# Biases of two mixtures of experts: from turned gates to a row of ones, a third output bank and a GpSimd add

## The reference, cut to what matters

```python
# first layer's mixture: 4 experts, 256 hidden, gates sum to 1 over two experts
for ei in range(4):
    g = jnp.where(topk_i == ei, w, 0.0).sum(-1)
    hh = gelu(x @ W1[ei] + b1[ei])
    out = out + g[..., None] * (hh @ W2[ei] + b2[ei])
...
# second layer's mixture: 8 experts, 256 hidden, two gates of eight are not zero
h = gelu(xf @ w1 + bb1)
y = h @ w2 + bb2
acc = acc + we[:, None] * y
```

## Time and profile before

| what | us |
|---|---|
| median of 3 runs (lowest 3353.7, highest 3367.92) | 3366.84 |
| the profiled execution | 3369.89 |
| its span, first to last instruction | 3368.1 |
| its front | 0 to 1171 |
| its last program | 1268 to 3368 |
| mean granted TensorE clock, share of full | 0.859 |

### The profile page before, as it was taken

One profiled execution on the slowest core, in us unless ns is written; L12 is line 12 of the kernel. 1 busy time (PEld: TensorE's weight loads), 2 busy tenths in 40 slices (PEclk: granted clock), 3 DMA queues, 4 the chain that ended last, 5 costly groups with the idle time before them and its releaser, 6 DMA issues.

```text
span 3368.1 us, 48945 instructions
## 1 busy us (share of the span) xinstructions
PE 2550.2 (76%) x15405; PEld 1888.7 (56%) x15406; DVE 2449.8 (73%) x7195; ACT 1767.8 (52%) x3180; POOL 1159.6 (34%) x1205
## 2 busy tenths in 40 slices
PE   1789898989889823026887887888878888887899
PEld 0666666767666612014555565665556556555666
DVE  6888888888878646246776866767777686676774
ACT  0566666676667502023555555555555555645654
POOL 0000000000000037656565565565555656556200
PEclk7899999999999955556898888888888988888899
DMA  2011111111111124133332333323233233332300
GB/s 92 32 51 45 54 47 49 54 41 45 47 45 45 53 76 98 34 72 73 79 76 63 85 71 64 91 64 86 66 71 89 63 86 70 81 75 64 83 14 10
DMA packets 228555, 210.48 MB, mean 62 GB/s; under 512 B 70780, under 2 KB 160584, under 8 KB 227656
## 3 DMA queue, kind: packets, MB, share of 16 engines
q1 hardware_dynamic: 190152, 190.84, 19.1%
q0 software_dynamic: 37280, 14.38, 4.8%
q10 hardware_dynamic: 864, 2.14, 0.2%
HBM read 159.49 MB, written 47.74 MB: 62 GB/s over the span
## 4 chain that ended last, share of the span: by engine, by line
DVE 23%; PE 17%; another core or an unknown queue 10%; issue 9%; ACT 3%; POOL 1%; DVEq 1%; DMA 0%; ACTq 0%; POOLq 0%
PE lay_b_y L1798 7%; DVE keep_x L2184 6%; PE lay_b_z L1789 6%; PE lay_b_b L1840 1%; POOL keep_got L1753 1%; DVE lay_oht L2089 1%; DVE lay_stats L2209 1%; ACT lay_unused L2031 1%; DVE lay_split L1093 1%; DVE lay_split L1094 1%; PE lay_b_g L1890 1%; DVE lay_oh L2086 1%; ACT lay_hid L1943 1%; DVE lay_split L1090 1%
## 5 line engine op out<-in xcount | busy, mean ns | idle before, releaser
L1753 POOL DMA_INDIRECT keep_got<-node_table,keep_idx x1143 | 1124.3, 984 | 765.3 <-issue 311.3
L1798 PEld LDWEIGHTS lay_b_y<-lay_w,lay_hid 128*128 128x128 f32 x4096 | 531.7, 203 | 170.2 <-issue 168.2
L1789 PE MATMUL lay_b_z<-lay_xin,lay_w 128*128 128x512 f32 x1024 | 584.9, 700 | 10.6 <-ACT lay_hid L1943 8.1
L1798 PE MATMUL lay_b_y<-lay_w,lay_hid 128*128 128x128 f32 x4096 | 544.4, 286 | 41.9 <-issue 39.1
L2184 DVE SCALAR_TENSOR_TENSOR keep_x<-lay_b_y,lay_gates,keep_x 128x128 f32<-128x128 f32 x1024 | 288.0, 343 | 380.4 <-remote 224.3
L1943 ACT ACTIVATE lay_hid<-lay_b_z,lay_b 128x512 f32<-128x512 f32 x512 | 330.3, 683 | 407.2 <-PE lay_b_z L1789 202.4
L902 POOL MEMSET find_ones<- 128x128 f32 x1 | 0.2, 205 | 1171.4 <-POOLq L49 1171.4
L2031 ACT ACTIVATE lay_unused<-keep_hub_wide,keep_halves 128x1152 bf16<-128x1152 uint16 x256 | 320.3, 1251 | 111.5 <-DMA keep_hub_wide<-sorted_dst 88.9
L1789 PEld LDWEIGHTS lay_b_z<-lay_xin,lay_w 128*128 128x128 f32 x1024 | 202.8, 220 | 178.7 <-issue 156.6
L468 PE MATMUL front_b_h<-front_xt,front_m 128*128 128x512 f32 x512 | 262.3, 643 | 38.2 <-DVE front_hb L719 32.0
L225 DVE TENSOR_TENSOR sort_keys<-sort_keys 128x1024 f32<-128x1024 f32 (+2 forms) x182 | 257.4, 1414 | 21.1 <-ACT sort_keys L548 18.3
(11 more groups left out here) (397 smaller groups left out, 4239.2 us busy)
## 6 DMA issues: line engine op xcount, KB each, us to landing
keep_wide<-sorted_dst SPq DMA_DIRECT2D x128, 288.0 KB
keep_hub_wide<-sorted_dst SPq DMA_DIRECT2D x128, 288.0 KB
made<-front_y SPq DMA_DIRECT2D x128, 256.0 KB, 2.0
lay_y<-made SPq DMA_DIRECT2D x32, 1024.0 KB
keep_got<-node_table,keep_idx POOLq DMA_INDIRECT x1152
front_adj<-in_adj SPq DMA_DIRECT2D x32, 256.0 KB, 3.1
keep_x<-in_x SPq DMA_DIRECT2D x32, 256.0 KB, 3.4
lay_adj<-in_adj SPq DMA_DIRECT2D x32, 256.0 KB
```

The costliest lines, as they stand in the source:

```text
L1753: pool.indirect_dma_start(out=got[:, b % RING, c, :], out_offset=None, in_=table, in_offset=bass.IndirectOffsetOnAxis(ap=idx[:, b % AHEAD, ...
L1789: pe.matmul(b_z[c][:, :], w1[:, e, P * c:P * c + P], flat(xin[g % 2][:, :, :]), start=True, stop=True).then_inc(z_done, 1)
L1798: mm = pe.matmul(b_y[n % 2][:, P * j:P * j + P], hid[n % 2][:, c, P * j:P * j + P], w2[:, e * HK + c, :], start=(c == 0), stop=(c == HK - 1))
```

## The change

The gates are no longer turned. The bank `b_b` becomes a third output bank, and the two kinds of bias enter in other ways:

- **Second mixture.** The biases are loaded three times, on three partitions. VectorE splits them once into three bfloat16 pieces whose sum is the float32 value (`bias_pieces`, in iteration 1). Each `down` begins with one more matmul, of the three pieces of its expert's bias under a row of ones (contraction over 3 rows, bfloat16, 512 columns); it sets the bank, and the eight products accumulate on it. VectorE's gated sum then carries the bias as well.
- **First mixture.** In the front, GpSimd subtracts 1 from the biases once and adds them to each stored expert output in SBUF, in place, between ScalarE's copy and SyncE's store. 128 such adds of 128x512 float32.
- `down` of expert n now waits for the outputs up to expert n - 3 only (`n - 2` in the code), over three banks; the turning, ScalarE's copies, the products and VectorE's adds of the gated biases (256, 64, 256 and 64 instructions of the program) are gone, with their semaphores.

```diff
+def bias_pieces(v, done, ident, biases, minus, pieces):
+    done.link(v.tensor_scalar(minus[:, 0:1], ident[0:PARTS, 0:1], -1.0, None, ALU.add))
+    done.link(v.tensor_tensor(minus[:, 1:2], minus[:, 0:1], ident[0:PARTS, 1:2], ALU.add))
+    for k in range(2):
+        done.link(v.tensor_copy(pieces[:, :, :], biases[:, :, :]))
+        done.link(v.scalar_tensor_tensor(out=biases[:, :, :], in0=pieces[:, :, :], scalar=minus[:, k:k + 1],
+                                         in1=biases[:, :, :], op0=ALU.mult, op1=ALU.add))
+    return v.tensor_copy(pieces[:, :, :], biases[:, :, :])
+def bias_product(pe, bank, ones, row):
+    pe.matmul(bank[:, :].rearrange("p (a b) -> p a b", a=TB), ones[:, :],
+              over(row.unsqueeze(1), [PARTS, TB, P]), start=True, stop=False)
...
 # front, SyncE
-                    sp.wait_ge(y_kept, n + 1)
+                    sp.wait_ge(y_biased, n + 1)
                     sp.dma_start(made[g, e, :, :], y[:, n % 2, :]).then_inc(y_stored[n % 2], 16)
+            sp.dma_start(mb2[:, :, :], w["mb2"].unsqueeze(0).broadcast_to([P, EXP, P])).then_inc(weights, 16)
...
 # front, GpSimd
+            pool.wait_ge(weights, 16 * 13)
+            pool.tensor_scalar(mb2[:, :, :], mb2[:, :, :], -1.0, None, ALU.add).then_inc(mb2_ready, 1)
+            pool.wait_ge(mb2_ready, 1)
+            for n in range(groups * EXP):
+                pool.wait_ge(y_kept, n + 1)
+                made_here = y[:, n % 2, :].rearrange("p (a b) -> p a b", a=TB)
+                pool.tensor_tensor(made_here, made_here, over(mb2[:, n % EXP, :].unsqueeze(1), [P, TB, P]), ALU.add)\
+                    .then_inc(y_biased, 1)
...
 # last program, TensorE
             def down(g, e):
                 n = g * E1 + e
+                if n == 0:
+                    pe.wait_ge(pieces_ready, 2)
+                if n == 2:
+                    pe.wait_ge(rest_counted, 1)
+                after(pe, y_added[1], n - 2)
+                bias_product(pe, b_y[n % 3], ones, pieces[:, e, :])
                 pe.wait_ge(hid_ready, HK * n + HK)
-                after(pe, y_added[1], n - 1)
                 for j in range(TB):
                     for c in range(HK):
-                        mm = pe.matmul(b_y[n % 2][:, P * j:P * j + P], hid[n % 2][:, c, P * j:P * j + P],
-                                       w2[:, e * HK + c, :], start=(c == 0), stop=(c == HK - 1))
+                        mm = pe.matmul(b_y[n % 3][:, P * j:P * j + P], hid[n % 2][:, c, P * j:P * j + P],
+                                       w2[:, e * HK + c, :], start=False, stop=(j == TB - 1 and c == HK - 1))
...
-                turn_gates(0, m)
                 attend(b)
...
-                bias(0, m)
...
-                turn_gates(1, f)
...
-                bias(1, f)
...
 # last program, ScalarE
-                keep_gates(0, m)
...
-                keep_gates(1, f)
...
 # last program, VectorE
-                    v.wait_ge(bias_added[0], g + 2)
+                    v.wait_ge(y_added[0], E0 * (g + 2))
...
-                    dense.link(v.tensor_scalar(b2[0][:, :], b2[0][:, :], -1.0, None, ALU.add))
+                    v.memset(ones[:, :], 1.0).then_inc(pieces_ready, 1)
+                    bias_pieces(v, dense, ident, biases, minus, pieces).then_inc(pieces_ready, 1)
...
-                bias(0, m)
...
-                bias(1, f)
```

More of the change, by code:

```diff
@@ L492, in _ @@
             turn_adj(0)
-            pe.wait_ge(weights, 16 * 12)
+            pe.wait_ge(weights, 16 * 13)
             aggregate(0)
@@ L1513, in layers @@
     n_edges = sorted_dst.shape[0] - GROUP
-    EXP = [a.shape[0] for a in w["b2"]]
+    EXP = [made.shape[1], w["b2"].shape[0]]
     H = w["W1"].shape[2]
@@ L1557, in layers @@
         b1 = s.sb("b1", [P, E1 * HK])
-        b2 = [s.sb(f"b2_{n}", [EXP[n], P]) for n in range(2)]
+        biases = s.sb("biases", [PARTS, E1, P])
+        minus = s.sb("minus", [PARTS, 2])
+        pieces = s.sb("pieces", [PARTS, E1, P], BF16)
+        ones = s.sb("ones", [PARTS, P], BF16)
         y0 = s.sb("y0", [P, 2, E0, N])
@@ L1592, in layers @@
         b_z = [s.bank(f"b_z{k}") for k in range(HK)]
-        b_y = [s.bank(f"b_y{k}") for k in range(2)]
-        b_b = s.bank("b_b")
+        b_y = [s.bank(f"b_y{k}") for k in range(3)]
+        b_rest = b_y[2]
         b_g = s.bank("b_g")
@@ L1708, in _ @@
                          allow_slow_non_contiguous=True).then_inc(weights, 16)
-            for n in range(2):
-                sp.dma_start(b2[n][:, :], w["b2"][n]).then_inc(weights, 16)
+            sp.dma_start(biases[:, :, :], w["b2"].unsqueeze(0).broadcast_to([PARTS, E1, P])).then_inc(weights, 16)
             for dst, src in ((b_gat[:, :], rows_of(w["b_gat"], HC)), (gamma[:, :], rows_of(w["ln_gamma"], HC)),
@@ L2190, in expert @@
                 ins.then_inc(y_added[n], 1)
-            def bias(n, g):
-                if not has(g):
-                    return
-                v.wait_ge(bias_done[n], g + 1)
-                v.wait_ge(y_added[n], EXP[n] * g + EXP[n])
-                v.tensor_tensor(x[:, of(g), :], x[:, of(g), :], b_b[:, :].rearrange("p (a b) -> p a b", a=TB),
-                                ALU.add).then_inc(bias_added[n], 1)
             def norms(g):
```

55 lines of the change are left out of this document (15 added, 40 removed).

## The result

The changed kernel takes 3420.81 us in the median of 4 runs (3413.1 to 3426.47) and the kernel before, beside it, 3365.8: ratio 1.0169 with a 95% interval of 1.0138 to 1.0201. It is slower, by 55 us between the medians and 57 us by the ratio. The forecast was 20 us faster. The profiled execution takes 3419.93 us, span 3418.2.

The account below looks back on a forecast made before the run. TensorE was taken to pace the front and the end, VectorE and TensorE half an iteration each between. Last program -38 and front +18 gave -20 us: 3350 us profiled, 3347 median; range 3272 to 3402.

Parts of the forecast that it names:

- The front: Stretch before the last program: 128 GpSimd adds of 1.1 us take VectorE's port at times; 18 us lost with one transfer.
- the cover at line 775: In the front, VectorE's wait there, 2.05 us on average in 20 of 32 groups, covers two adds of 1.1 us.
- 17 us: In the front, the loss from the other 12 groups, where VectorE is late already, 1.4 us each.
- The rival of the lock: In the front, GpSimd's adds take the port from VectorE's sort: 70 us lost, 3399 us in all; chance 0.22.
- the last program's -38: Sum for the last program: about 38 us gained, 40 of it from two bias adds removed in 25 iterations.
- VectorE's half: First part of an iteration, up to the normalised tile: VectorE sets the pace; two removed adds gain 1.6 us an iteration.
- The products: Last program, 256 matmuls of a row of ones: 0.26 us each at full clock, 33 to 133 us for all.
- TensorE's half: Rest of an iteration, expert after expert: 1.6 us removed, six products of 0.29 us added, nothing or 3 us lost.
- the sign of the tail: Last three iterations: eight products replace a turning and a product, 0.5 us lost in each; the final add goes, 1 gained.
- The 3 us gained ahead of the iterations: Last program, two or three iterations before experts run: the round trip of turning, copy and product falls out.
- TensorE bounds the whole iteration: Rival for the last program: TensorE's removed time counts too, some -105 us, with the front +18: 3280 us; chance 0.22.
- Handed back: Rival: the next late thing takes up VectorE's 1.6 us an iteration, front and last program cancel: 3365 us; chance 0.11.

Follow-up runs that it names:

- the one-column kernel: The changed kernel with its 128 GpSimd adds in the front cut from 512 columns to one; ratio to the kernel before 0.9946, once more 0.9911.

## Why the prediction was wrong, point by point

**The front was the step that failed.** The forecast gave 1.1 us for an add (measured 1.26 undisturbed), named the mechanism, and foresaw instructions stretched by up to 1.1 us: all of that is in the trace. Two steps failed.

The first is the sentence "The third and fourth fall on norms and on VectorE's wait for TensorE after them", to which it gave no cost. Counted by their place in the group, the first adds stretched VectorE by 31 us in the compared trace, the second by 21, the third by 23, the fourth by 19: the two that were put at nothing are 42 of some 94 us. The third add mostly falls on the ten small instructions at the norms' end, each waiting for the last, and there stands TensorE's wait for ScalarE's normalised tile: 20.8 us before in the front, 39.5 after.

The second is the cover at line 775, and with it the "17 us": the forecast let it take up 2.2 us in each of 20 groups, 44 us, and it took up 17 (38.9 us before from 105 us on, 22.2 after). VectorE's waits ahead of the banks' adds took up 11 more (58.1 before, 47.2 after), others 4: in all VectorE was 93 us longer busy from 105 us to the front's end and waited 32 less (169.8 before, 138.2 after). That is the 61.3 us, for 18 foretold.

The rival of the lock, "2.2 us in all 32 groups", 70 us, was right in kind and near in size, with a chance of 0.22. Its whole, 3399 us, was still too fast, since it took the last program's -38 as it stood. Of the 74 us between the median foretold and the one measured, 43 lie in the front and 27 in the last program; the rest is that the profiled execution lay 3 us over the median before and 1 us under it after.

**VectorE's half.** The wait at the normalised tile went, as said. Of 1.6 us an iteration, the first mixture's 0.8 was seen as 0.74 in the short condition. The second mixture's 0.8 did not come through: with its exchange the iteration stood at 50.49 us, with the first mixture's removal alone at 50.44. The steps there were 51.18 us before, 50.44 without the first mixture's biases, 48.76 without either, 50.49 with the products. Without the second mixture's turning, product and add 1.68 us went, where the forecast counts 0.8 + 1.6 = 2.4; TensorE's wait had moved to the edge block's split tile. That a removed 0.8 us counts in full held up to the next late thing.

**The products** were mis-sized a piece: 0.29 us in TensorE's half, measured 0.48 to 0.52 where nothing hides them. The row that the price came from, a one-hot product among its like the earlier trace rows, could not show what a bfloat16 product costs between float32 ones. The Trainium skill ("TensorE: Matmul & The Clock Gate", section on the back-to-back issue gap) gave 0.216 us for one; the second of two products, 0.2 us, agrees, the first does not. The forecast's upper bound for all 256, 133 us, is 0.52 each. For an iteration it was right all the same: 6 x 0.29 = 1.7 us foretold, 1.73 seen in the short condition. That is luck: eight at 0.48 would be 3.8, so more of them were covered than the two that the forecast left out, and the granted clock moved as well.

**The last program's -38** came out as -11.2 in the trace of the comparison, -13.4 in the short condition, and -22 and -35 in two more traces of the same last program in the long one (2176.0 and 2162.8 us for 2197.8, the only trace of the kernel before in that condition). So that term was too high in three of four and nearly reached in the fourth, and it isn't a constant: 24 us lie between three executions of one text of the last program, behind three different fronts.

**Right or nearly:** the third bank near 0 (some 6 us), the weights' transfer (1 us foretold, the first products start 1.9 us later), the split of the biases (eight instructions, not nine, 5.1 us in a row for the 2 taken; in the one-column kernel the stretch that holds them is 0.6 us longer than before), the sign of the tail (+3.7 us, for 1.5 foretold less 1). The 3 us gained ahead of the iterations did not come: that stretch grew by 4.6. **TensorE bounds the whole iteration** did not come. **Handed back** is what the second mixture's exchange did in the short condition. The prediction names for the adds at 2997.37 and 2997.97; they are in the earlier trace rows, and its 1.1 us for a pass of 1024 columns has no row (measured 0.68 us for a copy and 1.27 for a two-input pass).

## What to carry to other kernels

An engine that looks free is not free if another one has to wait for it: before giving GpSimd a two-input pass, list which of VectorE's instructions read two tensors of SBUF, count the pass at nearly its full length (here 1.1 of 1.26 us) against one that it meets, a small one as much as a long one, and start it beside bank reads or statistics instead. When a wait is moved, read the whole queue behind it (here one load: 149 us of waits). A price taken from a run of equal matmuls was too low here for a single one among others: 0.26 us foretold at the full clock, 0.48 to 0.52 measured. An estimate of an iteration can come out right by two errors, so take each of its terms from a run of its own.

## What the runs showed of the hardware that was not expected

- The lock is selective. Beside a GpSimd add of 1.26 us, VectorE's instructions with two SBUF tensors ended some 1.1 us late at any length (128x2048 and 128x8 alike), those with one operand in a bank and the batch statistics not at all (688 and 279 ns in means over 124 and 241). One-input instructions are between: 5 of the 8 small ones that started beside an add were stretched, by 0.2 to 1.0 us, and in the earlier trace rows a one-input copy of 512 columns lasted 2.54 us beside an iota of 2.28. The Trainium skill ("SBUF — State Buffer", section on the two sides of SBUF) names VectorE's two SBUF inputs as one condition of the lock; the trace agrees for 88 of 89. It names a mode of VectorE with two ports as the other, and no run here shows whether the stretched one-input instructions were in it. It also has the pair held for the whole GpSimd instruction; the two-input add comes near that (1.1 of 1.26 us), the one-input multiplication does not, which lasted 1.49 us and held VectorE for 0.3 to 0.45.
- A one-input GpSimd pass of 128x512 float32 took longer (1.49 us) than a two-input add of the same size (1.26), and cost the front a fifth as much (12.3 us for 61.6).
- The same kernel took 3090 or 3370 us, on one chip at different times, with granted clocks of 0.90 and 0.85 in the last program, and an edit that gained 26 us in the one condition lost 22 in the other.
- Less work on TensorE came with a lower granted clock in the iterations, twice: 0.90 to 0.85 without the products, 0.85 to 0.81 without the first mixture's biases in the long condition. No run shows which caused which.
